# Audio tower kernel: the q and v projections as fp32 products, their stores and the first attention loads on two queues

## The reference

```
h = tok(x)                                    # 8 rounds of two shifted 64x64 products
x = layernorm(h)                              # over the 64 features
v = (x @ wqv_w.T + wqv_b).reshape(b, t, 24, 64)
q, vf, vb = v[:, :, :8], v[:, :, 8:16], v[:, :, 16:]
k = x[:, :, None, :] * wk                     # 8 heads
a = -sum_w |q[s,h,:] - k[t,h,:]| / 8          # L1 scores
a = softmax over s, with one more row of zeros
o = (einsum('bsdh,bshw', a, vf) + einsum('bdsh,bshw', a, vb)).sum(heads)
h = h + (x + (o * sigmoid(1.702 o)) @ fanin_w.T + fanin_b)
h = h + ffn(layernorm(h))                     # 8 experts, the best 2
```

## Time and profile before

| | us |
|---|---|
| median of 3 runs | 8943.42 |
| lowest, highest | 8937.65, 8949.63 |
| profiled execution | 8950.86 |
| its span | 8949.1 |
| PE, ACT, DVE, POOL busy | 8741.1, 7728.7, 6953.8, 54.9 |
| token mixer, to the second block | about 102 |
| layer norm, q, v and their stores | 102 to 376 |
| attention's memsets and first loads | 376 to 411 |
| attention | 411 to about 8642 |
| feed-forward | the rest |

### The profile page before, as it was taken

One profiled execution on the slowest core, in us unless ns is written; L12 is line 12 of the kernel. 1 busy time (PEld: TensorE's weight loads), 2 busy tenths in 40 slices (PEclk: granted clock), 3 DMA queues, 4 the chain that ended last, 5 costly groups with the idle time before them and its releaser, 6 DMA issues. The chain is left out here.

```text
span 8949.1 us, 255296 instructions
## 1 busy us (share of the span) xinstructions
PE 8741.1 (98%) x115382; PEld 7003.0 (78%) x115382; DVE 6953.8 (78%) x5259; ACT 7728.7 (86%) x3721; POOL 54.9 (1%) x32
## 2 busy tenths in 40 slices
PE   7599999999999999999999999999999999999989
PEld 3279997989948987889968898688857888598863
DVE  3388888888888888888888888888888887888863
ACT  2299999999999999999989999999999999999965
POOL 1000000000000000000000000000000000000000
PEclk9799999999999999999999999999999999999989
DMA  2310000101010010100000010100001010000000
GB/s 79 123 17 2 17 2 2 17 2 17 2 17 2 2 17 2 17 2 17 2 10 8 2 17 2 17 2 17 2 2 17 2 17 2 17 2 2 2 12 8
DMA packets 134892, 114.72 MB, mean 13 GB/s; under 512 B 110954, under 2 KB 114474, under 8 KB 133530
## 3 DMA queue, kind: packets, MB, share of 16 engines
q1 hardware_dynamic: 133792, 98.00, 5.3%
HBM read 57.74 MB, written 40.22 MB: 11 GB/s over the span
## 5 line engine op out<-in xcount | busy, mean ns | idle before, releaser
L749 PE MATMUL sc<-ring,window 128*32 128x375 f32 x96000 | 7966.4, 478 | 1.7 <-DVE ring L870 1.7
L800 ACT ACTIVATE ring<-qx,xs 128x3000 f32<-128x3000 f32 x2624 | 7178.1, 2792 | 727.1 <-PE sc L749 726.2
L870 DVE TENSOR_SCALAR ring<-qx,xs 128x3000 f32<-128x3000 f32 x3376 | 6131.3, 1837 | 1478.9 <-PE sc L749 1405.0
L749 PEld LDWEIGHTS sc<-ring,window 128*32 128x32 f32 x96000 | 6124.6, 109 | 1306.6 <-issue 389.8
L722 PEld LDWEIGHTS acc<-ext,vf 128*32 128x32 f32 x9408 | 362.5, 109 | 38.2 <-issue 9.9
L709 PE MATMUL acc<-ex,vb 128*32 128x375 f32 x3088 | 382.9, 478 | 1.5 <-DVE ex L827 1.5
L722 PE MATMUL acc<-ext,vf 128*32 128x128 f32 (+1 forms) x9408 | 374.6, 270 | 0.2 <-DVE ext L835 0.2
L835 DVE STREAM_TRANSPOSE ext<-ex 128x768 f32<-128x768 f32 x385 | 374.1, 972 | 0.6
L785 ACT ACTIVATE ex<-sc 128x750 f32<-128x750 f32 x385 | 299.1, 777 | 5.6 <-PE sc L749 5.6
L738 PE MATMUL sc<-ksum,select 128*32 128x375 bf16 x3072 | 261.0, 324 | 33.8 <-DMA vf<-scratch_v 17.6
L738 PEld LDWEIGHTS sc<-ksum,select 128*32 128x32 bf16 x3072 | 187.1, 95 | 91.4 <-issue 33.8
(11 more groups left out here) (179 smaller groups left out, 1021.8 us busy)
## 6 DMA issues: line engine op xcount, KB each, us to landing
scratch_v<-vs SPq DMA_DIRECT2D x24, 1000.0 KB
qx<-scratch_qk SPq DMA_DIRECT2D x64, 375.0 KB
scratch_qk<-qs SPq DMA_DIRECT2D x32, 375.0 KB, 14.2
vb<-scratch_v SPq DMA_DIRECT2D x128, 92.0 KB
vf<-scratch_v SPq DMA_DIRECT2D x64, 184.0 KB
xs<-scratch_x SPq DMA_DIRECT2D x16, 187.5 KB
vb<-scratch_v SPq DMA_DIRECT2D x128, 1.8 KB
scratch_x<-xt SPq DMA_DIRECT2D x1, 1500.0 KB, 5.0
```

The lines of the kernel that those rows point to most:

```text
L749: mm = pe.matmul(bank[32 * j:32 * j + 32, h, 0:HALF], window[:, HALF_NH * g + j, ROWS - 1 - i:3 * ROWS - 1 - i], ring[:, slot, j, h * HALF ...
L800: act.activation(flat(ring[:, (HALF * g + k) % RING, :, :]), flat(qx[g][:, :, :]), ACT.Abs, bias=xs[g][:, 1, k:k + 1], scale=0.5).then_inc ...
L870: vec.tensor_scalar(flat(ring[:, (HALF * g + k) % RING, :, :]), flat(qx[g][:, :, :]), xs[g][:, 0, k:k + 1], xs[g][:, 1, k:k + 1], ALU.max, ...
```

## The change

What it does:

- q and v are one fp32 product of `w32` and `xt` for each half instead of six bf16 ones. The bf16 parts `wp` and `xp`, GpSimd's weight split and ACT's and DVE's splits of xt go.
- Attention's buffers (class `Attention`) are allocated before the token phase, and that phase borrows from them: `qs` lies in `qx[1]`, `vs` in `ext[0]`, `last` in `ext[1]`. `ks32` and `kparts` lie in `cen` and `sq`. All of these get other addresses.
- ACT issues each q store right after its eviction. SP keeps xt, ks and three of four v stores or more; chunks 5, 11, 17 and 23 are ACT's. The ks stores follow chunks 8, 10 and 12.
- GpSimd does the memsets in the second block, before its wait for xt; the clearing products read `oacc[:, 0, :]`.
- ACT issues pair 0's 30 loads at the end of its list in the second block, once the stores of sequence 0 have landed, and then the store of chunk 23. SP waits for all q and v stores in the attention block, before pair 1's loads. DVE waits for all v stores before it writes `ext[0]` at tile 1.

```
+            rows_v = scratch_v.rearrange("(b h k p) c -> b k p h c", b=B, h=2, k=PARTS)
...
+                    for c in range(NVC):
+                        if not on_act(c):
                             sp.wait_ge(v_made, 2 * c + 2)
+                            sp.dma_start(rows_v[c // PARTS, c % PARTS], vs[c % NVS]).then_inc(v_stored[c % NVS], 16)
+                        if c in (8, 10, 12):
...
-                        pe.wait_ge(x_third, ready_for(b))
+                        pe.wait_ge(x_made, ready_for(b))
...
+                            for h in range(2):
+                                mm = pe.matmul(pq[n % 2][:, h, 0:HALF], w32[64 * h:64 * h + 64, p * 128:(p + 1) * 128],
+                                               xt[64 * h:64 * h + 64, b * HALF:(b + 1) * HALF], start=True, stop=True)
...
+                    pool.memset(at.ksum[0][:, :], 0.0)
+                    pool.memset(at.vb[0][:, NT - 1, :], 0.0)
+                    pool.memset(at.vf[0][:, NBLK - 1, :], 0.0).then_inc(prepared, 1)
+                    pool.memset(at.ksum[1][:, :], 0.0)
+                    pool.memset(at.vb[1][:, :, :], 0.0)
+                    pool.memset(at.vf[1][:, :, :], 0.0)
+                    pool.memset(at.ex[0][:, :], 0.0)
+                    pool.memset(at.ex[1][:, :], 0.0)
+                    pool.memset(at.ext[1][:, :, :, :, :], 0.0)
+                    pool.memset(oacc[:, 0, :], 0.0)
                     pool.wait_ge(x_made, NQC)
...
+                    def store(n):
+
+                        act.wait_ge(q_made, n + 1)
+                        act.dma_start(scratch_qk[n, :, :], qs[n % NQS]).then_inc(q_stored[n % NQS], 16)
...
                     for b in range(1, B):
                         q(b)
+                        for c in range((b - 1) * PARTS, b * PARTS):
+                            if on_act(c):
+                                act.wait_ge(v_made, 2 * c + 2)
+                                act.dma_start(rows_v[c // PARTS, c % PARTS], vs[c % NVS]).then_inc(v_stored[c % NVS], 16)
+                    act.wait_ge(prepared, 1)
+                    act.wait_ge(xs_stored, 16)
+                    act.wait_ge(ks_stored, 96)
+                    for k in range(HP):
+                        act.wait_ge(q_stored[k], 16)
+                    for k in range(PARTS):
+                        act.wait_ge(v_stored[k], 16)
+                    at.load_pair(act, 0, 0, 0, scratch_x, scratch_qk, scratch_ks, scratch_v)
+                    c = NVC - 1
+                    act.wait_ge(v_made, 2 * c + 2)
+                    act.dma_start(rows_v[c // PARTS, c % PARTS], vs[c % NVS]).then_inc(v_stored[c % NVS], 16)
...
+                for k in range(NQS):
+                    sp.wait_ge(at.q_stored[k], 16 * len(range(k, B * HP, NQS)))
+                for k in range(NVS):
+                    sp.wait_ge(at.v_stored[k], 16 * len(range(k, NVC, NVS)))
...
+                with sp.Fori(0, B - 1) as b:
+                    load(b * 2 + 1, b, 1)
+                    load(b * 2 + 2, b + 1, 0)
+                load(NPAIR - 1, B - 1, 1)
...
                     vec.wait_ge(a_made, T + 3)
+                    if t == 0 and g == 0:
+                        for k in range(NVS):
+                            vec.wait_ge(at.v_stored[k], 16 * len(range(k, NVC, NVS)))
```

More of the change, by code:

```diff
@@ L37 @@
 SUB = EC // CH
+NLOADS = 2 + 4 + 4 * HALF_NH + 2 * HALF_NH
+NQS, NVS = HALF_NH, 3
+PARTS = HALF // CH
+NVC = B * PARTS
 PRODUCTS = ((0, 0), (0, 1), (1, 0), (1, 1), (0, 2), (2, 0))
@@ L78, in build, with phase_tokens @@
         select = sbuf(whole, "select", [128, 128], BF16)
-        phase_tokens(nc, A, sbuf, psum, semaphore, hx, oacc, window, select, scratch_x, scratch_qk, scratch_ks, scratch_v)
-        phase_attend(nc, sbuf, psum, semaphore, oacc, window, select, scratch_x, scratch_qk, scratch_ks, scratch_v)
+        with ExitStack() as middle:
+            at = Attention(middle, sbuf, semaphore)
+            phase_tokens(nc, A, sbuf, psum, semaphore, at, hx, oacc, window, select, scratch_x, scratch_qk, scratch_ks, scratch_v)
+            phase_attend(nc, sbuf, psum, semaphore, at, oacc, window, select, scratch_x, scratch_qk, scratch_ks, scratch_v)
         phase_feed(nc, A, out, sbuf, psum, semaphore, hx, oacc)
-def phase_tokens(nc, A, sbuf, psum, semaphore, hx, oacc, window, select, scratch_x, scratch_qk, scratch_ks, scratch_v):
+def phase_tokens(nc, A, sbuf, psum, semaphore, at, hx, oacc, window, select, scratch_x, scratch_qk, scratch_ks, scratch_v):
     with ExitStack() as ctx:
@@ L540, in _ @@
                     act.wait_ge(eps_set, 3)
-                    for c in range(NQC + 5):
+                    for c in range(NQC + 2):
                         if c < NQC:
@@ L545, in _ @@
                             root(c - 2)
-                        if 0 <= c - 4 < NQC:
-                            first(c - 4)
-                        if 0 <= c - 5 < NQC:
-                            second(c - 5)
                     act.wait_ge(signed_kept, 2)
@@ L574, in normal @@
                         vec.tensor_tensor(xt[:, cols(c)], cen[:, cols(c)], spread_bank(c), ALU.mult).then_inc(x_made, 1)
[L576 to L586 removed]
+                    for c in range(NQC + 3):
                         if c < NQC:
@@ L592, in _ @@
                             normal(c - 3)
-                        if 0 <= c - 5 < NQC:
-                            rest(c - 5)
-                        if 0 <= c - 6 < NQC:
-                            third(c - 6)
                     for c in range(NVC):
@@ L639, in phase_attend @@
         NPAIR = 2 * B
-        NLOADS = 2 + 4 + 4 * HALF_NH + 2 * HALF_NH
         NA = made_before(HALF, True)
@@ L648, in rows, with due @@
             return LROWS if t == NT - 1 else ROWS
-        def at(place, i, t):
+        def due(place, i, t):
             return i == min(place, rows(t) - 1)
@@ L882, in pair @@
                                     turn(T, n, 1 - g, NT - 1)
-                            if t == GROUP and at(KEEP_AT, i, t):
+                            if t == GROUP and due(KEEP_AT, i, t):
                                 keep(n, 1 - g, b + g)
```

206 lines of the change are left out of this document (76 added, 130 removed).

## The result

The changed kernel takes 8923.39 us (median of 13 runs, 8910.67 to 8932.44), the kernel before, timed with it, 8944.09 (13 runs); the ratio is 0.9972, 95% interval 0.9965 to 0.9979. It is faster by 0.28%, clear of the noise, but the forecast was 8895 and its range ended at 8914. The profiled execution took 8923.39 us, with a span of 8921.6.

A forecast was written before the change was run, and what follows sets the result against it. The prediction took v stores on five DMA engines to bound the store stage before attention. Its terms moved the first score product from 412.9 to 365 us, 48 us less, so 8943.4 became 8895 us; range 8868 to 8914.

The forecast's parts named there:

- front: Before the store stage: without the bf16 splits of xt, the first v store is issued 10.9 us earlier.
- q(7) stores: End of the store stage: the last batch's q stores, now on ACT's queue, go ahead of v20 and cost 4.2 us.
- loads' price on the v stores: First pair's loads, issued near 312 us beside v18 to v22, delay the v stores by 15 us (8 to 22.9).
- chunk 23 to the first product: Block change, PE's bank clearing (4.1 us) and select products (0.8) bring the first score product at 364.5 to 365.
- Products are worth nothing: Store stage: fewer products on PE save no time, since they hide behind the v stores.
- memsets cost nothing: Moved to GpSimd, memsets leave attention's start (12.5 us); price on DVE's norm stage 0 to 2 us, taken as 0.
- I take the same pace: Store stage: DVE's restarts from chunk 3 to chunk 23 keep their 185.7 us although ACT issues some v stores.
- v20 has landed, chunk 23, an issue, block change: Path to attention's start: v20 landed at 356.0, addition 2.35 us, issue 0.5, block change 0.7, start at 359.6.
- rival 1: End of store stage: the first loads finish only after v22, first score product 374.4 to 382, 8905 to 8913 us; chance 0.20.
- Rival 2: Store stage: five engines fed from two queues move more, so it shrinks, down to 8866 us; chance 0.18.
- Rival 3: Attention loop: new buffer addresses and DVE waits lengthen the tile, kernel slower at some 9145 us; chance 0.04.
- DVE's new wait at tile 1: Attention: DVE waits for all v stores before tile 1's transpose at 402; they land near 380, cover 22 us.

The follow-up runs named there:

- e4: Kernel before with the fp32 products alone, no bf16 splits; stores, memsets and loads as before: 8934.9 us, ratio 0.9986.
- e2: Changed kernel with all q and v stores issued by SP in the order of before, first loads still on ACT: 8915.7 us, ratio 0.9964.
- e6: Changed kernel with the first pair's 30 loads issued by SP in the attention block, after all stores: 8932.0 us, ratio 0.9983.
- e3: Changed kernel with each v store split in two, rows 0 to 111 and 112 to 124: 8813.1 us, ratio 0.9851.
- e8: Kernel before with each v store split into rows 0 to 111 and 112 to 124, nothing else: 8838.6 us, ratio 0.9876.
- e7: Changed kernel with every fp32 product of q and v made twice: 8914.5 us, ratio 0.9962.
- e1: Changed kernel with all 24 v stores issued by SP, q stores and first loads still on ACT: 8917.5 us, ratio 0.9967.
- e10: The same kernel as e1, run again: 8914.2 us, ratio 0.9959.
- e12: Changed kernel with the six ks stores issued by GpSimd on its own queue instead of by SP: 8919.5 us, ratio 0.9971.
- e11: Changed kernel with each v store split into rows 0 to 111 and 112 to 124, all on SP: 8815.0 us, ratio 0.9848.
- e5: Changed kernel with 11 of the 24 v stores on ACT's queue instead of 4: 8920.7 us, ratio 0.9967.

## Why the prediction was wrong, step by step

The forecast can be put in the same terms: 262.2 us from the block's start to the first product, against 286.6.

| step | forecast | measured | from |
|---|---|---|---|
| before, to chunk 23's addition | 244.9 | 244.9 | before |
| front | -10.9 | -11.4 | e4 |
| two queues (forecast: only the q(7) stores) | +4.2 | +19.8 | after less e2 |
| loads' price on the v stores | +15 | +6.4 | e2 less e4 |
| chunk 23 to the first product | +9 | +26.9 | after |
| sum | 262.2 | 286.6 | |

How the two middle terms share their sum depends on the order in which they are taken out: by e6, which is after without the early loads, the loads cost 2.8 us and the queues 23.4.

**Bound and front: right.** v stores on five engines bound the stage; the split (e3, e8) proves it. The first v store is issued at 137.8 (141 forecast, 151.89 before); the 7 us DVE step is gone. Products are worth nothing (e7), memsets cost nothing: GpSimd's run from 102.71 to 113.8, and the reciprocal at 112.01 still takes 0.20 us beside the longest of them (ext, 5.22 us from 108.21). That agrees with the Trainium skill, "SBUF — State Buffer" (Who interferes with whom), by which a DVE instruction with at most one SBUF input, outside the two-port modes, does not contend with GpSimd. No DVE instruction with two SBUF inputs ran beside these memsets, so the rule that the prediction named was not put to the test.

**"I take the same pace": wrong, and the first step that failed.** 182.1 us for 156.7 (chunk 3 to 20), and the q(7) stores, for which the working had allowed 4.2 us, have no part in that: they are issued from about 332 on, when chunk 20 has restarted (331.59). e2 has the pace with the new products and one queue. e1 and e10 give the shares: some 6 to 10 us for the q stores' own queue, 15 to 18 for v stores on two. The working had read "every fifth to sixth is only issued by ACT", as if an issuing engine were a label. What lies behind the second share: packets that take longer, an estimated 6 to 8 us (e12's section), and engines out of step; how much the second costs, and whether the ks hold has a part in it, was not measured by itself. In after chunk 10's store is on SP's queue and chunk 11's on ACT's. DVE waits 18.76 us for the first and not at all for the second: by their semaphores they have landed at 269.61 and 270.81, though the second was issued some 7 us after the first, and on three of the five engines chunk 10 was through by 247.32. The Trainium skill, "DMA: Bandwidth & Descriptors" (Queues, rings and completion order), says that an engine takes turns between its queues packet by packet. That would let two stores of two queues land together; the trace fits it on the engines that were last (262.53 and 269.61 for chunk 10, 264.43 and 270.81 for chunk 11), and no run shows why these had fallen behind.

The prediction leaned on the rule of the Trainium skill, "DMA: Bandwidth & Descriptors" (Rules for kernel authors), that spreading DMAs over several issuing engines doesn't help bandwidth, and took it as "no change". No run speaks against the rule. It leaves open that it can cost: for v stores on two queues 15 to 18 us of pace here on five engines, and nothing clear on sixteen (e3 and e11).

**The loads: price too high, place wrong.** I priced them at 15 us on the v stores. They cost 6.4 (2.8 by e6), below the lower end of 8. But they are not through when the v stores that they run beside have landed: ACT issues them for 43.6 us, in e2 for 59.4 and in e1 for 55.3, where 17.0 suffice alone (e6). The block ends when ACT's list does. So "v20 has landed, chunk 23, an issue, block change" was the wrong path: 18 us of waiting for the end of ACT's list stand there, and that term alone is 17.9 of the 24.4 us by which the sum was off. It is rival 1 ("if ACT's are held up as well"), and e2, which has its premises (pace as before), came out at 8915.7 where that rival said 8905 to 8913. Against it I had put "separate queues, and 11 engines that v stores leave alone". The 11 didn't help: the issues were held up on ACT's queue all the same, until the v stores were nearly or wholly through. Which engines held them was not shown; a load that also uses a busy engine would be as late as that engine, and its issue hold all that follow.

The two errors don't add up, since late loads hide behind late stores. With the pace of e2 and the loads held up as they were, 13.9 us of the 24.4 are left (276.1 less 262.2); the queues add the other 10.5.

**Rival 2** (two queues move more) is refuted by e1, e10 and e12: v stores on two move less. **Rival 3** is refuted by every run: 8528 to 8540 us from the first product to the end, tile 22.10 us, L807 at 2792 ns. DVE's new wait at tile 1 costs nothing: its transpose starts at 427.63, 38.7 us after the first score product, and the last v store, issued at 382.06, has landed at 392.34 by its semaphore. That is a cover of 35 us; 22 were forecast.

**In the median.** The trace's 24.0 us are 20.7 in one comparison and 29.1 (8947.12 less 8918.05) in the other; a gain of about 21 to 29 us, and 48 in neither.

## What to carry to other kernels

An issuing engine is part of a transfer's cost. Before moving DMAs to a second queue, ask whether the DMA engines that they use are full: here the move gained nothing, lost 15 to 18 us in 180, and held up the issuing engine, so that the block that ended with its list ended late. Where a share like 0.32 says that five of sixteen engines do all the work, look at the partition count first: splitting 125 rows into 112 and 13 was worth 110.1 us by itself (e8 against before), four to five times what the whole change was.

## What the runs showed of the hardware that I had not expected

- At the same share of 0.32, v stores on one queue move 129 to 131 GB/s, and on two 123 to 124 in two windows of e12; a 4096-byte packet takes 162 to 166 ns and 172.
- 30 loads of 3.28 MB take their engine 17.0 us to issue when the DMA engines are idle (e6), 27.9 us beside stores on sixteen engines (e3), 39.0 (e7) to 59.4 us (e2) beside stores on five. Single issues reach 7.48 us (e5).
- The five engines of a store can finish it far apart: 2.7 us on average in before, 10 in after, up to 25 (chunk 10, 244.77 to 269.61). The store on the other queue behind it landed 1.2 us later.
- The second block starts between 96.0 and 102.8 us in the profiled executions, whatever the edit: 7 us that a single profile would mix with the effect of the change, and the reason to count from the block's start.
